# An embedding tower: the second chunk's gathers released by the split instead of the turned copy, and one later lookup placed a tile later

## What is computed

```python
e = stack([tbl_f[ids[:, f]] for f in range(39)], axis=1)      # (512, 39, 16)
x1 = einsum('bid,bjd,ijh->bhd', e, e, W0.reshape(39, 39, 128))
x2 = einsum('bid,bjd,ijh->bhd', e, x1, W1.reshape(39, 128, 128))
z = sum(concatenate([x1, x2], axis=1), axis=-1)               # (512, 256)
h = maximum(concatenate([z, dense_ctx], axis=1) @ W_top1 + b_top1, 0)
h = maximum(h @ W_top2 + b_top2, 0)
y = h @ W_top3
```

## Time and profile before

| | |
|---|---|
| median of 3 runs | 233.53 us |
| the profiled execution | 233.34 us |
| its span, first to last instruction | 231.4 us |
| what lies around the span | 1.9 us |
| TensorE matmul busy | 215.8 us, 93% |
| VectorE busy | 164.3 us, 71% |
| ScalarE busy | 160.0 us, 69% |
| GpSimd busy | 98.6 us, 43% |

### The profile page before, as it was taken

The page is one execution under the profiler, slowest core; times in us unless marked ns, Lnnn a source line. Parts: engine busy times, 40 slices in busy tenths (PEclk is TensorE's granted clock), DMA queues, the critical chain, the costliest instruction groups (busy, mean ns, idle before and its releaser), DMA issues.

```text
span 231.4 us, 4819 instructions
## 1 busy us (share of the span) xinstructions
PE 215.8 (93%) x1717; PEld 172.2 (74%) x1717; DVE 164.3 (71%) x347; ACT 160.0 (69%) x319; POOL 98.6 (43%) x99
## 2 busy tenths in 40 slices
PE   4489799997889999999999999999999999999996
PEld 4378367674566578988787788887876788887995
DVE  3989988967598996977869996866587855561101
ACT  3996889797769786598685957787668585663201
POOL 4774377777557787750667777600000000000000
PEclk9979999999799999999999999999999999999999
DMA  4991009914000000000000000000000000000000
GB/s 122 243 305 21 3 11 284 260 13 94 6 7 7 7 9 6 10 6 0 9 5 7 9 7 9 6 1 3 0 0 4 0 0 3 0 0 3 0 0 3
DMA packets 7579, 8.57 MB, mean 37 GB/s; under 512 B 2631, under 2 KB 5164, under 8 KB 7556
## 3 DMA queue, kind: packets, MB, share of 16 engines
q1 hardware_dynamic: 4516, 7.48, 11.9%
q0 software_dynamic: 3040, 0.78, 3.5%
HBM read 8.25 MB, written 0.00 MB: 36 GB/s over the span
## 4 chain that ended last, share of the span: by engine, by line
PE 78%; DVE 5%; DMA 4%; issue 4%; POOL 3%; ACT 3%; SPq 1%; DVEq 0%; ACTq 0%
PE turn_bank L607 16%; PE x_bank L536 9%; PE pair_bank L508 8%; PE x_bank L539 8%; PE x_bank L538 8%; PE g_bank L570 5%; POOL emb L478 3%; PE misc_bank L570 3%; PE g_bank L587 3%; PE turn_bank L645 3%; PE x_bank L550 3%; DMA emb<-tbl,ids_sb 2%; PE turn_bank L618 2%; DMA tab<-small 2%; PE pair_bank L735 1%
## 5 line engine op out<-in xcount | busy, mean ns | idle before, releaser
L478 POOL DMA_INDIRECT emb<-tbl,ids_sb x95 | 98.4, 1035 | 50.5 <-ACT prod L1047 22.0
L1047 ACT ACTIVATE prod<-pair_bank 128x512 f32<-128x512 f32 (+1 forms) x108 | 64.6, 605 | 38.7 <-PE pair_bank L508 38.7
L897 DVE TENSOR_TENSOR prod_lo<-prod,prod_hi 128x512 fp32r<-128x512 f32 x92 | 61.6, 684 | 9.7 <-ACT prod_hi L1052 8.8
L536 PE MATMUL x_bank<-prod_hi,pair_w_hi 128*128 128x512 f32 (+1 forms) x108 | 60.5, 560 | 1.7 <-DVE prod_lo L897 1.0
L508 PE MATMUL pair_bank<-x,sel 117*128 117x512 bf16 (+1 forms) x112 | 42.2, 386 | 2.2 <-ACT prod L1047 1.4
L607 PEld LDWEIGHTS turn_bank<-g_sb,w_sb 128*128 128x128 f32 x312 | 40.0, 191 | 3.4 <-issue 1.0
L607 PE MATMUL turn_bank<-g_sb,w_sb 128*128 128x128 f32 x312 | 42.3, 278 | 0.0
L1052 ACT ACTIVATE prod_hi<-prod 128x512 fp32r<-128x512 f32 x64 | 40.8, 638 | 0.2
L538 PE MATMUL x_bank<-prod_lo,pair_w_hi 128*128 128x512 f32 x92 | 36.9, 401 | 0.0
L539 PE MATMUL x_bank<-prod_hi,pair_w_lo 128*128 128x512 f32 x92 | 36.9, 401 | 0.0
L885 DVE CAST prod_hi<-prod 128x512 fp32r<-128x512 f32 x44 | 18.5, 421 | 16.5 <-ACT prod L1047 16.4
(11 more groups left out here) (147 smaller groups left out, 304.0 us busy)
## 6 DMA issues: line engine op xcount, KB each, us to landing
emb<-tbl,ids_sb POOLq DMA_INDIRECT x95, 2.4
tab<-small SPq DMA_DIRECT2D x2, 560.0 KB
wt<-w_top SPq DMA_DIRECT2D x2, 512.0 KB
tab<-small SPq DMA_DIRECT2D x1, 504.0 KB
wa<-pair_w_a SPq DMA_DIRECT2D x1, 448.0 KB
wb<-pair_w_b SPq DMA_DIRECT2D x1, 448.0 KB
wtd<-w_dense SPq DMA_DIRECT2D x1, 256.0 KB
dense_sb<-dense_t SPq DMA_DIRECT2D x1, 256.0 KB
```

The lines of the kernel that those rows point to most:

```text
L478: pool.indirect_dma_start(out=emb[:, at:at + D], out_offset=None, in_=tables[f], in_offset=bass.IndirectOffsetOnAxis(ap=ids_sb[:, c * M + ...
L536: mm = pe.matmul(x1_banks[k % 2][:, :], pair_w_hi[p, t, :], hi(n), start=(t == 0), stop=(t == FULL))
L897: dve.tensor_tensor(lo(n), prod[rows, n % RING, :], prod_hi[rows, n % RING2, :], ALU.subtract).then_inc(lo_done, 1)
L1047: act.activation(prod[0:ROWS[t], n % RING, :], pair_bank[n % 2][0:ROWS[t], :], ACT.Square).then_inc(sq_done, 1)
```

## The change

It has two parts. GpSimd no longer waits for the three copies of the first chunk's turned x before it starts the second chunk's gathers; it waits until the three pieces of that x are split. And the lookup of part 0 of the second chunk stands in step 5 in place of step 4, on each engine; its one-hot rows stand in steps 0, 0, 1, 2, 3 in place of 0, 0, 0, 1, 2.

```diff
         def look_step(c, part):
-            return ((c - 1) * NB + part + (c > 1 and PARTS[c] < 3)) * NT + LOOK_AT
+            return ((c - 1) * NB + part + (c > 1 and PARTS[c] < 3)) * NT + LOOK_AT + (nth(c, part) == 0)
...
             for c in range(NCH):
                 if c == 1:
-                    pool.wait_ge(x3_a, 2)
-                    pool.wait_ge(x3_b, 1)
+                    pool.wait_ge(split_done, pieces(0))
                 for f in range(first_gathered(c), M):
```

## The result

| | before | changed |
|---|---|---|
| median of 20 runs each | 234.68 us (232.79 to 236.25) | 233.00 us (231.91 to 235.10) |
| the profiled execution | 233.34 us | 232.75 us |
| its span | 231.4 us | 230.9 us |

The ratio to before is 0.9941, with a 95% interval of 0.9918 to 0.9965: a small gain. With more runs the median of before came out 1.15 us higher than in the first three, and its runs spread over 3.5 us. So the medians are 1.68 us apart, and the two profiled executions only 0.59: the profiled one of before is among its faster ones.

A forecast was written before the change was run, and what follows sets the result against it. GpSimd's gathers were taken to bound the first chunk's end, with most of the span TensorE's own work. 233.34 - 1.93 (earlier gathers) + 0 (lookup) + 1.3 (slower clock) = 232.7 us, range 231.2 to 233.8.

The forecast's parts named there:

- The bound: End of the first chunk: GpSimd's 27 gathers, 26.07 to 61.69 us, set when the second chunk's turn starts.
- The wait on GpSimd: Before the second chunk's gathers: GpSimd released 1.94 us earlier, so gathers and the second chunk's turn come 1.93 us earlier.
- The gathers' durations: Second chunk's gathers, 0.94 to 1.64 us each: no contention taken; gain 2.6 if the 27th is short, 1.3 with contention.
- The landing: 20th gather, used 3.3 us after its end, w_top2's data taken as cause: lands about 51.7, before that data moves.
- first stall: ScalarE standing from 54.13 to 55.40 us for the 20th gather (1.27 us); claimed to go entirely.
- The lookup: First chunk's tiles: moving the lookup a tile later lets them run 0.3 to 1.2 us ahead, 0.65 taken.
- this part is worth 0 at the end: The lookup's lead of 0.65 us is hidden, since ScalarE waits 1.15 us for the 27th gather anyway.
- The clock: Start of the second chunk: 3.1 us of idle TensorE, then half clock for about 3.4 us, costing 1.3 us (0.9 to 1.7).
- Rival 1: Second chunk's start: clock holds or falls only inside the idle time, gain of 1.93 kept, 231.4 us; chance 0.28.
- Rival 2: Second chunk's start: clock stays low for two stretches, 62.8 to 69.5, costing 3.2 us, 234.6 us; chance 0.08.
- The time: Whole kernel: 232.7 us from the profiled 233.34; chance 0.41 of over 0.5% faster, 0.52 within, 0.07 slower.

The follow-up runs named there:

- early kernel with filler: Changed kernel, GpSimd not waiting before the second chunk's gathers, pacing five squares looser, 8 unused matmuls in TensorE's idle time: 229.84 us, ratio 0.9803; at 264 us 1.0184.
- release alone: Changed kernel with the lookup left in step 4, so only GpSimd's wait differs from before: 234.1 us, ratio 0.9972; in the set at 264 us 0.9956.
- The filler: Changed kernel plus 12 matmuls with unused result in TensorE's idle time before the second chunk's turn: 231.55 us, ratio 0.987; at 264 us 0.9891.

## Why the prediction was right, and where it was off

The mechanism held in the profiled executions: the wait on GpSimd gave 1.9 us, and the clock took most of it back. Three things were off, the effect of the lookup, the idle time as the sole cause of a slow clock, and the size of the gain against the typical run of before.

- **The bound.** The gathers end the first chunk: shown by the early kernel with filler, where their earlier start takes the turn to 61.23 and ScalarE's wait goes, and by the lookup alone, where the turn came with the last gather and not with the tiles.
- **The wait on GpSimd.** Forecast: third gather at 26.71, 27th ending at 59.8, turn at 62.3. Measured: 26.52, 59.86, 62.41. The first gather came 0.27 us behind its release, not 0.78, and it made no difference, since the square holds the third.
- **The gathers' durations.** The 27th took 0.94 us, not 1.64, but others stretched in its place (one took 1.61). The stretching moves: from the third's start to the 27th's end were 33.05 us before, 33.34 in the changed kernel, 33.96 with the release alone. What stretches a gather was not found. That the full 1.9 us came out owes something to luck: with the release alone it was 1.07. VectorE's copies were not what does it: the two gathers beside them in the changed kernel (23.44 and 24.69) took 0.94 and 0.95 us.
- **The landing.** The 20th gather landed in time and the first stall went, as forecast. That w_top2's data had caused the late landing was not tried by itself.
- **The lookup.** VectorE's first `take_lo` came at 28.35 and the tiles ran ahead as forecast. But the step "this part is worth 0 at the end" failed where it stands alone: 1.0055. The tiles' lead was hidden, as forecast. What I had left out is that the gathers' durations differ from execution to execution by about as much as the whole lead, and that 0.9 us more of them lengthens TensorE's idle time, behind which the clock then fell. Why the kernel is slower in most runs stays open beyond that one execution. Whether the lookup is behind the difference between 0.9972 and 0.9941 can't be said, since the intervals overlap.
- **The clock.** Forecast: 3.1 us of idle TensorE, then half clock, 1.3 us given back (0.9 to 1.7). Measured: 3.29 us, half clock from 61.9 to 65.2, 1.38 us given back; 1.67 and 1.65 in the other two kernels that showed it. That the middle of the range fitted is luck of position: the clock fell 0.5 us before the turn in the changed kernel, and 0.2 and 0.6 us behind its start in the other two, where the slow stretch lay wholly over work. The filler took it away and brought 1.1 us of span. But the forecast's ground, that idle time as long as that is punished, is too simple: the clock held behind 3.49 and 3.28 us in two heads. Rival 1 had a real chance, and the changed kernel's 20 runs, none with a mean clock of 1.00, are the better ground for saying that it seldom comes true. Rival 2's ground against it, that slow stretches lasted only 3.3 to 3.4 us, doesn't hold either: in the head of the early kernel with 8 filler matmuls one lasted from 10.0 to 16.9.
- **The time.** Forecast 232.7, against 232.75 in the profiled execution and a median of 233.0. Against the median of before over 20 runs the gain is 1.7 us, 1.4 by the ratio, and so somewhat above the half per cent that I gave 0.52 to stay within. The profiled execution of before, from which I worked, is among its faster ones. The forecast gain was 0.6 us, which is what the profiled pair shows; taken from the median of before it would give 234.0, a microsecond too much. So part of the closeness of 232.7 to 233.0 is luck, and what makes the typical run of before slower than the profiled one stays open. A slower clock behind the turn can't be all of it: in the first set at 235 us one run of before took 234.81 us at a mean granted clock of 1.00. The kernel without idle time before its turn had all its runs between 229.63 and 230.24.

## What to carry to other kernels

When a wait is shortened on one engine, add up what TensorE's idle time becomes, not only when its work begins: here 1.9 us of earlier start bought 0.5, because half the clock was lost for 3.3 us behind 3.3 us of idle. Idle time that can't be removed can be filled with matmuls whose result nobody uses, if they end before the awaited data comes; 12 of them were worth 1.1 us of span. One profiled execution doesn't settle what the clock does; the mean granted clock of many runs says more. And an edit whose lead is hidden behind a wait isn't sure to be free, as the lookup alone shows with 0.6% more time, so the parts of a pair should be tried alone as well as together.

## What was new about the hardware

- The clock fell behind 3.29 us of idle TensorE (changed kernel), 3.26 (release alone), 2.56 (lookup alone), 1.90 (release alone at 264 us) and 1.5 us in two pieces, and held behind 3.49 us and 3.28 (heads of the 12 fillers and of the release alone), 1.92 (lookup alone at 264 us) and 1.37 (before). So the length of the idle time alone doesn't say whether it falls. Where it fell behind the turn it stayed at 0.50 for 3.3 to 3.4 us; in one head it did so for 6.8 us (early, 8 filler matmuls).
- The transposes follow the clock like other matmuls: the first five took 0.46 us at 1.00 and 0.76 at 0.50.
- A gather of 128 rows took 0.94 us, or up to 1.6, with 0.30 us between two of them; the longer ones stood at other places in each profiled kernel.
- The same program took 235 us or 264, by the set of runs. At 264 ScalarE paused for 8.3 us in the head, and for 18.4 with more gathers issued there, and the fastest kernel at 235 us is among the slowest at 264. An early start of gathers should be judged in both.
